# LoRA's transpose behind the output projection, norms 1 and 2 scaled on ScalarE, router logits earlier on VectorE, another form for the row maxima's products

## The chip, the cores and the metric

The kernel runs on one core of a Trainium2 chip. The metric is the device time in microseconds of one execution; lower is better. A core has TensorE (matrix products into PSUM), VectorE, ScalarE and GpSimd (elementwise work; the profile calls them PE, DVE, ACT and POOL), and SyncE (SP), which here issues the DMAs. Each engine runs its own instructions in the order in which they were written, and semaphores tie the engines together.

## The reference

Two layers of cross attention, each followed by a feed-forward part, over x of 8 tiles of 128 tokens by 512. A context of the same size is given. Cut to what matters:

```
x = x + tanh(g0) * xattn_L0(layernorm(x), ctx)     # norm 0; 32 heads, 8 kv heads of 128, rms norm of q and k
x = x + tanh(g1) * lora_ffn(layernorm(x))          # norm 1
x = x + tanh(g2) * xattn_L1(layernorm(x), ctx)     # norm 2; 16 heads, 4 kv heads of 96
x = x + tanh(g3) * swiglu_ffn(layernorm(x))        # norm 3

def lora_ffn(x):                                   # 8 experts of rank 16
    scores = 8 * softmax(x @ Wr.T + br)
    low = einsum('bsd,hrd->bshr', x, A)
    return 2 * einsum('bshr,hor,bsh->bso', low, B, scores)
```

The attention is softmax(q k^T / sqrt(d)) v over 256 keys (128 of the context, 128 of x itself), then the output projection Wo. All is asked for in float32. The kernel keeps the accuracy by splitting each operand into two float16 pieces, high and low, and making three products of them.

## The kernel before

**Tiles and steps.** A group is one kv head pair's share of the weights with NH = 4 query heads; layer 0 has 8 groups and layer 1 has 4, each over the 8 token tiles. That makes N = 96 steps n, 64 of layer 0 (N0) and 32 of layer 1. Each engine has its own function `step(n)`, called in a loop. A pass n works on three steps at once: k, v and q are projected for step T = n + 3; scores, maxima, exponentials and the two pieces of the probabilities are made for S = n + 1; the values product is made for n; the output projection is made for Y = n - 1 (n - 2 in layer 1).

**What runs beside.** `beside(n)` says which tile's norms and LoRA ride along in pass n: norm 1 of tile n - 58, LoRA of tile n - 59, norm 2 of tile n - 60. So LoRA runs in passes 59 to 66, norm 1 in 58 to 65, norm 2 in 60 to 67. Passes 59 and 60 still project for layer 0 (with sums of squares on ScalarE for the rms norms), the ones from 61 on for layer 1.

**A norm.** VectorE takes the statistics (`norm_stats`, L1088 and L1090), GpSimd makes `var_e` and `rstd` (L1473, L1469), VectorE scales `xn` = (x - mean) rstd (`norm_scale`, L1100). For norms 1 and 2 ScalarE copies `xn` into a float16 row tile `n_rows` (`norm_row_hi`, L806), GpSimd puts the rest beside it (`norm_rows`, L1486), and a DMA transposes both into `xT` (`turn_norm`).

**LoRA in a pass.** TensorE projects into bank 2 (`lora_project`, activations and router logits). VectorE makes logits with bias and their maximum (`router_logits`: `lg`, `lmx`), ScalarE the exponential (`router_exp`), VectorE the scaled activations `lora_act` (`lora_scale`, L1235). TensorE transposes them (`lora_turn`, L666), ScalarE and VectorE split the result into `tT_hi` and `tT_lo` (`lora_act_hi`, `lora_low`), TensorE multiplies by B (`lora_project_out`) and VectorE adds to x (`lora_add`, L1246). Bank 2 is the only one for this, so the next pass's `lora_project` waits for `lora_add`.

**Row maxima.** `row_max(n, i)` on VectorE takes the negated maximum over two heads' scores (`mx`, L1180) and multiplies the two columns by a scale into `nb` (L1185 in layer 0, L1189 in layer 1). ScalarE's exponentials (`exps`, L900) use `nb` as bias. VectorE then inverts the sums (`sums_in`, `rs`), and the high and low pieces follow (`probs_high` on ScalarE, `probs_low` on VectorE, `pieces`).

The order of the work is the written order of the calls in each `step(n)`; nothing reorders it.

## Time and profile before

| | us |
|---|---|
| median of 3 runs | 1193.6 |
| lowest, highest | 1191.94, 1197.27 |
| profiled execution, its own time | 1195.74 |
| profiled execution, span | 1193.9 |
| passes before the norms 1 and LoRA come in, one pass of layer 0 | 10.4 |

The page gives for this span: TensorE busy 1133.5 us (95%), VectorE 853.4, ScalarE 825.9, GpSimd 368.6; mean granted TensorE clock 0.986. Busy time alone doesn't say which engine ends a stage, since the engines overlap. What an engine waited for, how long, and what it did in what order tells that; these rows stand further down.

### The profile page before, as it was taken

What the parts mean: (1) busy time and instruction counts of PE and PEld (TensorE: products, weight loads), DVE (VectorE), ACT (ScalarE), POOL (GpSimd) and SP (SyncE); (2) the same over time, 40 slices, a digit from 0 to 9 for tenths busy, and PEclk for the clock granted to TensorE, in tenths of its full rate; (3) what the DMA queues carried; (4) which work ended last, traced back from release to release, by engine and by line L of the source; (5) the groups of instructions that cost most, each with busy time, mean ns of one, the idle gap of its engine ahead of it and who ended that gap; (6) DMA issues with size and microseconds to landing.
All of it is one profiled execution on the core that took longest, in us unless ns stands there. A gap on an engine that the chain in (4) does not pass through costs nothing.

```text
span 1193.9 us, 22716 instructions
## 1 busy us (share of the span) xinstructions
PE 1133.5 (95%) x7184; PEld 712.3 (60%) x7184; DVE 853.4 (71%) x2066; ACT 825.9 (69%) x2695; POOL 368.6 (31%) x668
## 2 busy tenths in 40 slices
PE   6789999999999999999999977899999999799998
PEld 4445666666666666666666544566676766455554
DVE  5578767767777677677676888898887888843434
ACT  5678878888888888878778865577777675522221
POOL 5555333335633333333333543321211121100000
PEclk8899999999999999999999999999999999999999
DMA  6466654464655644555545645568987786200000
GB/s 241 105 141 119 129 137 103 120 137 85 148 123 128 129 101 121 119 109 127 141 95 115 129 96 124 126 136 164 236 182 148 139 159 131 56 1 1 36 1 36
DMA packets 411993, 139.56 MB, mean 117 GB/s; under 512 B 386657, under 2 KB 396641, under 8 KB 411873
## 3 DMA queue, kind: packets, MB, share of 16 engines
q1 hardware_dynamic: 409968, 134.43, 51.1%
q0 software_dynamic: 1904, 3.67, 1.1%
q8 instruction: 58, 0.95, 0.3%
q14 instruction: 63, 0.51, 0.2%
HBM read 39.21 MB, written 2.10 MB: 35 GB/s over the span
## 4 chain that ended last, share of the span: by engine, by line
PE 75%; DVE 9%; SPq 4%; issue 4%; ACT 3%; POOL 3%; DMA 1%; DVEq 0%; POOLq 0%; ACTq 0%
PE bank L517 21%; PE bank L519 21%; PE bank L518 21%; PE bank L718 8%; PE bank L737 4%; SPq L420 1%; DVE mx L1180 1%; DVE stats L1088 1%; ACT probs L900 1%; POOL rstd L1469 1%; DVE pieces L1077 1%; SPq L443 1%; DMA turned<-pieces 1%; SPq L426 1%; SPq L432 1%
## 5 line engine op out<-in xcount | busy, mean ns | idle before, releaser
L806 ACT ACTIVATE pieces<-probs,rs 128x256 f16<-128x256 f32 x384 | 165.3, 524 | 10.6 <-DVE rs L1195 8.4
L1180 DVE TENSOR_REDUCE mx<-bank 128x2 f32<-128x512 f32 x192 | 131.5, 685 | 56.6 <-PE bank L519 56.5
L900 ACT ACTIVATE probs<-bank,nb,rq 128x256 f32<-128x256 f32 x256 | 141.3, 564 | 39.1 <-DVE nb L1185 38.6
L1077 DVE SCALAR_TENSOR_TENSOR pieces<-probs,rs,pieces 128x256 f16<-128x256 f32 x384 | 162.6, 485 | 5.5 <-ACT pieces L806 5.3
L517 PE MATMUL bank<-wo_hi,oT 128*128 128x512 f16 x352 | 135.9, 386 | 6.3 <-DVE oT L1077 4.8
L517 PE MATMUL bank<-wq,xT 128*128 128x512 f16 (+1 forms) x384 | 139.3, 363 | 2.7 <-DVE wq L1077 2.7
L809 ACT ACTIVATE junk<-bank 128x128 bf16<-128x128 f32 x384 | 102.1, 289 | 53.9 <-PE bank L519 53.8
L518 PE MATMUL bank<-wq,xT 128*128 128x512 f16 (+1 forms) x384 | 138.9, 362 | 0.0
L519 PE MATMUL bank<-wq,xT 128*128 128x512 f16 (+1 forms) x384 | 138.7, 361 | 0.0
L519 PE MATMUL bank<-wo_hi,oT 128*128 128x512 f16 x352 | 135.8, 386 | 0.0
L518 PE MATMUL bank<-wo_lo,oT 128*128 128x512 f16 x352 | 135.7, 385 | 0.0
L1077 DVE SCALAR_TENSOR_TENSOR q_rows<-bank,q_rows 128x512 f16<-128x512 f32 (+1 forms) x96 | 61.2, 638 | 79.0 <-ACT junk L809 79.0
L517 PE MATMUL bank<-wkv,xT 128*128 128x256 f16 (+1 forms) x384 | 102.0, 266 | 5.3 <-DVE xT L1074 2.2
L517 PE MATMUL bank<-wkv,cT_hi 128*128 128x256 f16 (+1 forms) x384 | 103.2, 269 | 2.9 <-DVE cT_lo L1077 2.9
L517 PE MATMUL bank<-k_half,q_half 128*128 128x256 f16 (+1 forms) x384 | 105.1, 274 | 0.1
L519 PE MATMUL bank<-k_half,q_half 128*128 128x256 f16 (+1 forms) x384 | 105.2, 274 | 0.0
L518 PE MATMUL bank<-k_half,q_half 128*128 128x256 f16 (+1 forms) x384 | 105.1, 274 | 0.0
L718 PE MATMUL bank<-xT,ff_in 128*128 128x512 f16 x448 | 101.5, 380 | 3.4 <-DVE xT L1074 2.2
L518 PE MATMUL bank<-wkv,cT_hi 128*128 128x256 f16 (+1 forms) x384 | 103.2, 269 | 0.0
L519 PE MATMUL bank<-wkv,cT_lo 128*128 128x256 f16 (+1 forms) x384 | 103.0, 268 | 0.0
L519 PE MATMUL bank<-wkv,xT 128*128 128x256 f16 (+1 forms) x384 | 102.2, 266 | 0.0
L518 PE MATMUL bank<-wkv,xT 128*128 128x256 f16 (+1 forms) x384 | 102.1, 266 | 0.0
(184 smaller groups left out, 2640.7 us busy)
## 6 DMA issues: line engine op xcount, KB each, us to landing
raw_o<-in_wo_a SPq DMA_DIRECT2D x8, 1024.0 KB, 6.1
raw_q<-in_wq_a SPq DMA_DIRECT2D x7, 1024.0 KB, 5.9
raw_kv<-in_wkv_a SPq DMA_DIRECT2D x8, 512.0 KB, 3.9
turned<-pieces SPq DMA_TRANSPOSE x192, 2.8
raw_q<-in_wq_c SPq DMA_DIRECT2D x4, 768.0 KB, 5.1
raw_o<-in_wo_c SPq DMA_DIRECT2D x4, 768.0 KB, 5.1
down_rest<-in_down_t POOLq DMA_DIRECT2D x5, 512.0 KB, 4.2
ff_in<-in_gate_t SPq DMA_DIRECT2D x4, 448.0 KB, 3.9
```

What stands on the lines that cost most here:

```text
L420: sp.dma_start_transpose(turned_in[:, n % 2, i], halves[:, i, :]).then_inc(pturned[i], 16)
L426: sp.dma_start_transpose(q_half[n % 2], q_rows[:, :]).then_inc(qturned, 16)
L517: pe.matmul(out, w[0], m[0], start=start, stop=False)
L518: pe.matmul(out, w[0], m[1], start=False, stop=False)
L519: return pe.matmul(out, w[1], m[0], start=False, stop=stop)
L718: last = pe.matmul(out[:, :], w[:, k, m * P:(m + 1) * P], xT[i][:, k, toks], start=k == 0 and i == 0, stop=k == KC - 1 and i == 1)
L737: last = pe.matmul(bank[t][:, :], hT[n % 2][i][:, t * P:(t + 1) * P], down_w(m), start=m == 0 and i == 0, stop=m == MT - 1 and i == 1)
L806: return act.activation(out, in_, ACT.Copy, scale=scale)
L809: return act.activation(out, in_, ACT.Square, scale=scale, accum_out=total)
L900: act.activation(probs[:, h, :], bank[h // 2][:, (h % 2) * KV:(h % 2 + 1) * KV], ACT.Exp, bias=nb[:, h:h + 1], scale=scale, accum_out=sums ...
L1077: return dve.scalar_tensor_tensor(out, in_, scale, hi, ALU.mult, ALU.subtract)
L1180: dve.tensor_reduce(mx[:, pr], chunks(bank[i][:, :], 2), AX.X, ALU.max, negate=True).then_inc(mx_done, 1)
```

## The change

Four things, all in the calls of the passes and in the helpers they use.

1. TensorE: `lora_turn` stands behind `project(Y)`, no longer ahead of it. ScalarE's `lora_act_hi` and VectorE's `lora_low` move behind the first half of the probabilities' pieces.
2. VectorE: LoRA's logits come before norm 3's scaling (in no pass do both occur), `lora_scale` between the two row maxima and no longer behind both.
3. Norms 1 and 2: VectorE scales them no more. GpSimd makes `shift` = -mean rstd, and ScalarE computes x rstd + shift twice, into `xn` (float32) and into the float16 row tile. Norm 1 stands ahead of norm 2 on GpSimd and in the DMA queue. On ScalarE norm 1's scaling stands right behind `o_hi`, norm 2's behind the router's exponential.
4. `nb` is made with a SCALAR_TENSOR_TENSOR: times 1.0 and times `rq` in layer 0; times `es` plus a tile of zeros in layer 1. This holds for all 192 products.

```diff
@@ TensorE, step
                 if norm3 is not None:
                     norm_turn(3, norm3)
+                if Y is not None:
+                    project(Y)
                 if lora is not None:
                     lora_turn(lora)
-                if Y is not None:
-                    project(Y)
                 values(n)
@@ ScalarE
-            def norm_row_hi(k, t):
-                act.wait_ge(norm[k].xn, t + 1)
+            def norm_scaled(k, t):
+
+                act.wait_ge(norm[k].shift, t + 1)
                 if t >= 1:
+                    act.wait_ge(norm[k].row_lo, t)
                     act.wait_ge(norm[k].moved, 16 * t)
-                copy(rows_slot(k)[:, 0:D], xn[xn_slot(k, t)]).then_inc(norm[k].row_hi, 1)
+                for out, done in ((xn[xn_slot(k, t)], norm[k].xn), (rows_slot(k)[:, 0:D], norm[k].row_hi)):
+                    act.activation(out, xt[:, t, :], ACT.Identity, bias=shift[:, t:t + 1], scale=rstd[:, t:t + 1]
+                                   ).then_inc(done, 1)
@@ ScalarE, step
                     o_hi(n - 1)
+                if norm1 is not None:
+                    norm_scaled(1, norm1)
                 g = kv_squared(n)
...
-                if norm2 is not None:
-                    norm_row_hi(2, norm2)
-                if norm1 is not None:
-                    norm_row_hi(1, norm1)
                 if lora is not None:
                     router_exp(lora)
+                if norm2 is not None:
+                    norm_scaled(2, norm2)
                 if S < N:
                     exps(S, 0)
...
-                if lora is not None:
-                    lora_act_hi(lora)
                 if norm3 is not None:
                     norm_hi(3, norm3)
                 if S < N:
                     probs_high(S, 0)
+                if lora is not None:
+                    lora_act_hi(lora)
+                if S < N:
                     probs_high(S, 1)
@@ VectorE, row_max
-                    dve.tensor_tensor(nb[:, pr], mx[:, pr], rq[:, c:c + 2], ALU.mult).then_inc(nb_done, 1)
+                    dve.scalar_tensor_tensor(nb[:, pr], mx[:, pr], 1.0, rq[:, c:c + 2], ALU.mult, ALU.mult
+                                             ).then_inc(nb_done, 1)
...
-                    dve.tensor_scalar(nb[:, pr], mx[:, pr], es[:, g % 2, s:s + 1], None, ALU.mult).then_inc(nb_done, 1)
+                    dve.scalar_tensor_tensor(nb[:, pr], mx[:, pr], es[:, g % 2, s:s + 1], zeros[:, :], ALU.mult, ALU.add
+                                             ).then_inc(nb_done, 1)
@@ VectorE, step
-                if norm1 is not None:
-                    norm_scale(1, norm1)
-                if norm2 is not None:
-                    norm_scale(2, norm2)
-                if norm3 is not None:
-                    norm_scale(3, norm3)
                 if lora is not None:
                     norms_of_step(n)
                     router_logits(lora)
+                if norm3 is not None:
+                    norm_scale(3, norm3)
                 if S < N:
                     row_max(S, 0)
                 if lora is None:
                     norms_of_step(n)
+                if lora is not None:
+                    lora_scale(lora)
                 if S < N:
                     row_max(S, 1)
-                if lora is not None:
-                    lora_scale(lora)
...
-                if lora is not None:
-                    lora_low(lora)
                 if norm3 is not None:
                     norm_low(3, norm3)
                 if S < N:
                     probs_low(S, 0)
+                if lora is not None:
+                    lora_low(lora)
+                if S < N:
                     probs_low(S, 1)
@@ GpSimd, norm_rstd
                 power(rstd[:, t:t + 1], var_e[:, t:t + 1], half_neg[:, 0:1]).then_inc(norm[k].rstd, 1)
+                if k in (1, 2):
+                    pool.wait_ge(norm[k].rstd, t + 1)
+                    pool.tensor_scalar(shift[:, t:t + 1], moments[:, 2 * t:2 * t + 1], rstd[:, t:t + 1], -1.0,
+                                       ALU.mult, ALU.mult).then_inc(norm[k].shift, 1)
```

Left out are the tiles `shift` and `zeros` with the semaphore `shift`, and the exchange of the calls for norms 1 and 2 on GpSimd and SyncE.

VectorE in pass 61, before, from the end of LoRA's addition in pass 60 on (`x<-bank,tg_lora,x` stands just ahead; `xn` are norms 1 and 2, `mx` and `nb` the row maxima and their products):

```order
L1088 BN_STATS stats<-x 128x6
L1090 BN_AGGR moments<-stats 128x2
L1077 SCALAR_TENSOR_TENSOR oT<-bank,oT 128x512
L1100 TENSOR_SCALAR xn<-x,moments,rstd 128x512 x2
L1114 TENSOR_SCALAR nrm<-bank 128x2
L1223 SCALAR_TENSOR_TENSOR lg<-bank,l_inv,bias_r 128x8
L1226 TENSOR_REDUCE lmx<-lg 128x1
L1180 TENSOR_REDUCE mx<-bank 128x2
L1185 TENSOR_TENSOR nb<-mx,rq 128x2
L1180 TENSOR_REDUCE mx<-bank 128x2
L1185 TENSOR_TENSOR nb<-mx,rq 128x2
L1231 RECIPROCAL lrs<-lsum 128x1
```

and the same place in the changed kernel:

```order
L1084 SCALAR_TENSOR_TENSOR oT<-bank,oT 128x512
L1119 TENSOR_SCALAR nrm<-bank 128x2
L1230 SCALAR_TENSOR_TENSOR lg<-bank,l_inv,bias_r 128x8
L1233 TENSOR_REDUCE lmx<-lg 128x1
L1185 TENSOR_REDUCE mx<-bank 128x2
L1190 SCALAR_TENSOR_TENSOR nb<-mx,rq 128x2
L1238 RECIPROCAL lrs<-lsum 128x1
L1240 TENSOR_SCALAR lg<-lg,lrs 128x8
L1242 TENSOR_TENSOR lora_act<-bank,lg 128x128
L1185 TENSOR_REDUCE mx<-bank 128x2
L1190 SCALAR_TENSOR_TENSOR nb<-mx,rq 128x2
```

The two scalings are gone, the activations' scaling stands one row maximum earlier, and `nb` has the other form.

ScalarE in pass 61, before (`n_rows` are the copies of norms 2 and 1, `probs` the attention's exponentials):

```order
L806 ACTIVATE oT<-bank 128x512
L806 ACTIVATE v_hi<-bank,alpha 128x96 x2
L806 ACTIVATE n_rows_51<-xn 128x512
L806 ACTIVATE n_rows_50<-xn 128x512
L925 ACTIVATE lg,lsum<-lg,lmx 128x8
L900 ACTIVATE probs,sums<-bank,nb,rq 128x256 x4
L806 ACTIVATE q_rows<-bank 128x4x96
L806 ACTIVATE tT_hi<-bank 128x128
L806 ACTIVATE pieces<-probs,rs 128x2x128 x4
```

and in the changed kernel:

```order
L808 ACTIVATE oT<-bank 128x512
L824 ACTIVATE xn<-x,shift,rstd 128x512
L824 ACTIVATE n_rows_50<-x,shift,rstd 128x512
L808 ACTIVATE v_hi<-bank,alpha 128x96 x2
L931 ACTIVATE lg,lsum<-lg,lmx 128x8
L824 ACTIVATE xn<-x,shift,rstd 128x512
L824 ACTIVATE n_rows_51<-x,shift,rstd 128x512
L906 ACTIVATE probs,sums<-bank,nb,rq 128x256 x4
L808 ACTIVATE q_rows<-bank 128x4x96
L808 ACTIVATE pieces<-probs,rs 128x2x128 x2
L808 ACTIVATE tT_hi<-bank 128x128
L808 ACTIVATE pieces<-probs,rs 128x2x128 x2
```

Two copies have become two pairs, norm 1's ahead of `v_hi`, norm 2's between the router's exponential and the attention's; `tT_hi` is now between the halves of the pieces.

## Rows read from the trace of the kernel before

**Rows 1.** Busy time by window, passes before norm 1; columns: us, busy of each engine, clock.

```profile
core 0: us, PE busy (x) PEld busy (x) DVE busy (x) ACT busy (x) POOL busy (x), PEclk, DMA share, GB/s
96.00:656.80 560.80, 559.74 (x3584) 347.98 (x3585) 404.03 (x1013) 463.41 (x1670) 223.36 (x389) 1.00 0.54 120
```

**Rows 2.** The same view, windows from one LoRA addition's end to the next.

```profile
689.24:704.94 15.70, 11.62 (x82) 7.12 (x82) 13.15 (x33) 11.24 (x41) 7.06 (x12) 1.00 0.44 99
704.94:720.33 15.39, 11.95 (x76) 7.06 (x77) 12.51 (x34) 7.21 (x20) 6.00 (x10) 0.89 0.42 95
720.33:734.87 14.54, 11.63 (x93) 7.74 (x91) 12.89 (x33) 10.02 (x28) 4.66 (x8) 1.00 0.56 145
734.87:749.77 14.90, 11.46 (x70) 6.51 (x71) 12.35 (x31) 7.59 (x22) 4.66 (x8) 0.89 0.44 99
749.77:764.75 14.98, 12.55 (x87) 7.83 (x85) 11.91 (x32) 7.17 (x21) 5.67 (x10) 0.89 0.43 98
764.75:777.17 12.42, 9.62 (x86) 7.02 (x84) 10.81 (x30) 8.47 (x24) 4.65 (x8) 1.00 0.66 140
777.17:788.47 11.30, 9.49 (x71) 6.29 (x72) 10.68 (x28) 7.66 (x25) 2.79 (x5) 1.00 0.59 132
```

**Rows 3.** Waits between 678 and 790 us: who for whom, total, times, longest.

```profile
PE bank L666 <- DVE lora_act L1235: 19.1, 7, 3.4
...
DVE xn L1100 <- POOL rstd L1469: 8.2, 7, 1.3
```

**Rows 4.** VectorE's timeline, passes 60 to 61: start, length, instruction, idle before.

```profile
701.43 0.74 DVE L1215 SCALAR_TENSOR_TENSOR x<-bank,ty,x 128x512 f32<-128x512 f32 x1
...
703.54 0.74 DVE L1077 SCALAR_TENSOR_TENSOR wo_lo<-raw_o,s_o,wo_hi 128x512 f16<-128x512 f32 x1
704.20 0.74 DVE L1246 SCALAR_TENSOR_TENSOR x<-bank,tg_lora,x 128x512 f32<-128x512 f32 x1
...
705.71 0.18 DVE L1090 BATCH_NORM_AGGREGATE moments<-stats 128x2 f32<-128x6 f32 x1
705.81 0.66 DVE L1077 SCALAR_TENSOR_TENSOR oT<-bank,oT 128x512 f16<-128x512 f32 x1
707.77 1.00 DVE L1100 TENSOR_SCALAR xn<-x,moments,rstd 128x512 f32<-128x512 f32 x2 [1.30 <-POOL rstd L1469]
...
709.01 0.16 DVE L1226 TENSOR_REDUCE lmx<-lg 128x1 f32<-128x8 f32 x1
...
709.80 0.97 DVE L1185 TENSOR_TENSOR nb<-mx,rq 128x2 f32<-128x2 f32 x1
...
712.26 0.29 DVE L1235 TENSOR_TENSOR lora_act<-bank,lg 128x128 f32<-128x128 f32 x1
...
713.37 0.16 DVE L1193 TENSOR_SCALAR sums_in<-sums 128x4 f32<-128x4 f32 x1
...
714.39 1.67 DVE L1077 SCALAR_TENSOR_TENSOR pieces<-probs,rs,pieces 128x256 f16<-128x256 f32 x4
```

**Rows 5.** ScalarE's timeline, pass 61.

```profile
708.81 1.15 ACT L806 ACTIVATE n_rows<-xn 128x512 f16<-128x512 f32 x2 [4.46 <-DVE xn L1100]
709.87 0.28 ACT L925 ACTIVATE lg<-lg,lmx 128x8 f32<-128x8 f32 x1
...
710.81 0.56 ACT L900 ACTIVATE probs<-bank,nb,rq 128x256 f32<-128x256 f32 x1 [0.57 <-DVE nb L1185]
```

**Rows 6.** GpSimd's timeline, pass 61.

```profile
706.26 0.56 POOL L1469 TENSOR_TENSOR rstd<-var_e,half_neg 128x1 f32<-128x1 f32 x1
...
709.61 2.27 POOL L1486 TENSOR_TENSOR n_rows<-xn,n_rows 128x512 f16<-128x512 f32 x2 [1.87 <-ACT n_rows L806]
```

**Rows 7.** Timelines of VectorE and GpSimd near 69 us, where they overlap.

```profile
68.84 2.65 DVE L1077 SCALAR_TENSOR_TENSOR wo_lo<-raw_o,s_o,wo_hi 128x512 f16<-128x512 f32 x2
...
69.47 1.48 POOL L1486 TENSOR_TENSOR n_rows<-xn,n_rows 128x512 f16<-128x512 f32 x1
```

**Rows 8.** ScalarE's timeline, pass 60.

```profile
690.67 0.62 ACT L806 ACTIVATE v_hi<-bank,alpha 128x128 f16<-128x128 f32 x2
...
695.10 0.56 ACT L900 ACTIVATE probs<-bank,nb,rq 128x256 f32<-128x256 f32 x1 [0.54 <-DVE nb L1185]
```

More of the change, by code:

```diff
@@ L119, in __init__ @@
             self.row_hi = sem("row_hi")
+            self.shift = sem("shift")
             self.row_lo = sem("row_lo")
@@ L206, in build @@
         half_neg = sb("half_neg", NT)
+        zeros = sb("zeros", 2)
         half_pos = sb("half_pos", NT)
@@ L213, in build @@
         stats, moments = sb("stats", NT * 6), sb("moments", NT * 2)
-        var_e, rstd = sb("var_e", NT), sb("rstd", NT)
+        var_e, rstd, shift = sb("var_e", NT), sb("rstd", NT), sb("shift", NT)
         ssq = sb("ssq", C_SUM + len(SETS), BF16)
@@ L451, in step @@
                     turn_norm(0, norm0)
+                if norm1 is not None:
+                    turn_norm(1, norm1)
                 if norm2 is not None:
                     turn_norm(2, norm2)
-                if norm1 is not None:
-                    turn_norm(1, norm1)
                 if T < N:
@@ L946, in step @@
                     o_hi(n - 1)
+                if norm1 is not None:
+                    norm_scaled(1, norm1)
                 g = kv_squared(n)
@@ L1093, in norm_scale @@
                 dve.wait_ge(norm[k].rstd, t + 1)
-                if k in (1, 2) and t >= 1:
-                    dve.wait_ge(norm[k].row_lo, rows_before(k, t))
                 if k in (0, 3) and t >= 2 and turned_by_dma(k, t - 2):
@@ L1272, in step @@
                     context_low(norm0)
-                if norm1 is not None:
-                    norm_scale(1, norm1)
-                if norm2 is not None:
-                    norm_scale(2, norm2)
-                if norm3 is not None:
-                    norm_scale(3, norm3)
                 if lora is not None:
@@ L1612, in step @@
                 next0 = beside(n + 1)[0]
+                if norm1 is not None:
+                    norm_rstd(1, norm1)
                 if norm2 is not None:
                     norm_rstd(2, norm2)
-                if norm1 is not None:
-                    norm_rstd(1, norm1)
                 if norm3 is not None:
@@ L1620, in step @@
                     norm_rows(0, norm0)
+                if norm1 is not None:
+                    norm_rows(1, norm1)
                 if norm2 is not None:
                     norm_rows(2, norm2)
-                if norm1 is not None:
-                    norm_rows(1, norm1)
                 if T < N0:
@@ L1662, in _ @@
             pool.memset(both_half[:, 1:2], 0.5).then_inc(consts, 1)
+            pool.memset(zeros[:, :], 0.0).then_inc(consts, 1)
             pool.memset(kb[:, :], XS * XS * RMS_EPS * L0.hd).then_inc(consts, 1)
@@ L1665, in _ @@
             norm_rstd(0, 1)
-            pool.wait_ge(consts, 8)
+            pool.wait_ge(consts, 9)
             kv_scale(0)
```

## The prediction

> **What bounds the kernel now.** I read the busy time by stage first. Between 96 and 656.8 us TensorE is busy 559.7 of 560.8 us [rows 1]: there the other engines follow, and an edit on them is worth nothing unless it makes TensorE wait. The stretch with LoRA is different. It has eight passes of the step loop, n = 59 to 66. I cut it where LoRA's result has been added (end of the `x<-bank,tg_lora,x` row, L1246), the point that the next pass needs before bank 2 is free. That gives seven lengths, 15.70, 15.39, 14.54, 14.90, 14.98, 12.42 and 11.30 us, together 99.2 [rows 2]. TensorE is busy 78.3 of these, part of that at half clock: the granted clock is 0.89 in three of the seven (2.4 GHz for most of the pass, 1.2 for the rest). So this is the stretch in which 99 us can shrink, and the rest of the kernel offers nothing.
>
> The waits say where it goes [rows 3]: TensorE sat 19.1 us before the transpose of `lora_act` (L666), in seven waits, and VectorE 8.2 us before `xn` for GpSimd's `rstd`. The order on VectorE in pass 61 [rows 4] shows why: after LoRA's addition ends at 704.94 come `oT` (705.81), a wait and the two scalings of norms 1 and 2 (707.77, 1.00 us), the router logits (`lmx` at 709.01), a maximum, the product `nb` (709.80, 0.97 us), and `lora_act` only at 712.26. ScalarE's exponentials of the attention start at 710.81 [rows 5], 5.87 us after the cut. Everything that ends the pass (`pieces`, the output's addition, weights, LoRA's addition) hangs on them and on VectorE's queue.
>
> **The change part by part,** laid out for pass 61 with 704.94 as zero.
>
> (a) VectorE loses the two scalings and the wait ahead of them. After `oT` ends (705.81 + 0.66, so 1.53) the logits and their maximum follow directly. Now they take from the end of `xn` (708.77) to that of `lmx` (709.17), 0.4 us: `lmx` is ready at 1.95. The row maximum needs the first half of the scores. By their shapes at 2.4 GHz LoRA's projection (12 products of 136 columns) takes 0.68 us and half of the scores (6 of 256) 0.64, so they are there by 1.4 to 1.8, in time.
>
> (b) GpSimd: norm 1 goes ahead of norm 2 and each gets one more instruction (`shift`, estimated at 0.3, half of `rstd`'s 0.56). Norm 1's moments are there before the cut. Norm 2's end at 0.95 (705.71 + 0.18 [rows 4]); `rstd` followed by 706.82 [rows 6], so `shift` stands at 2.2. That costs nothing, since ScalarE is busy until then.
>
> (c) ScalarE: the two copies (1.15 us for two, [rows 5]) become two pairs, 2.30. Norm 1's pair runs before `v_hi`, while ScalarE waits anyway. Norm 2's pair stands ahead of the exponentials: router exponential 2.0 to 2.45 (0.28 us and the reading of its sum, [rows 5]), pair 2.45 to 3.6, exponentials from 3.65 instead of 5.87. Identity with two operands per row has no row here; I take the copy's 0.57 each, bounds 0.5 and 0.8 (the second would add 0.5 us a pass).
>
> (d) `nb`. The 0.97 us in [rows 4] is not work: GpSimd's `n_rows` runs from 709.61, 2.27 us for two [rows 6], and `nb` ends with the first. Does the new form escape that? The nearest rows of SCALAR_TENSOR_TENSOR with both inputs in SBUF say no: two `wo_lo` took 2.65 us at 68.84, where one takes 0.74 [rows 4], beside an `n_rows` of 1.48 [rows 7]. So I expect the new form to wait too: the first product ends with norm 1's `n_rows` (GpSimd free for it at 2.2, so near 3.35), hidden behind the scaling pair on ScalarE (3.6). For the 176 products outside the stretch I take 0, since TensorE's own work covers them there [rows 1]; if the cover were gone, each could be longer or shorter by some 0.05. The zeros' memset at the start is behind the load of x: 0.
>
> The trace has the old `nb` held by GpSimd, and held rows of the new form as well. The Trainium skill, "SBUF — State Buffer", section "Who interferes with whom", says that a VectorE instruction with two SBUF inputs contends with a GpSimd instruction that reads SBUF, whatever the opcode; that speaks against this part of the change, and the trace's `wo_lo` agrees. By it the sum stays as it is; were only the old form held, some 3.5 us more would go.
>
> (e) LoRA's scale: now before the second maximum. It needs ScalarE's router exponential (2.45) and VectorE past the first `nb` (3.35); three short instructions, the last of 0.29 [rows 4], estimated at 0.75 together: `lora_act` done at 4.1, the second maximum and `nb` to 5.0, `v_lo` and `kn` to 5.9. The four exponentials end at 3.65 + 4 x 0.56 = 5.9. The two chains meet, neither waits for long.
>
> (f) TensorE: the output projection no longer stands behind the transpose. By the shapes it runs 4.0 to 6.6 at full clock (12 products of 512 columns) and the transpose follows with `lora_act` long there, so that wait goes whole. What is late next: LoRA's last product, now behind `tT_lo`, which has been put behind the first two `pieces`. From `sums_in` to the end of the four `pieces`, `tT_lo` among them, took 713.37 to 716.06, 2.7 us; started at 5.95 and with 0.2 for ScalarE's lead it ends at 8.9, `tT_lo` at 8.05; the product then ends at 8.8 and `v`, `k` of the next pass at 10.8. TensorE then waits about half a us for the addition: VectorE sets the length.
>
> (g) The tail on VectorE, from the y addition to the end of LoRA's: 701.43 to 704.94 is 3.5 us in pass 60, of which `wo_lo` 0.66 (703.54 to the next start) and a `wq` of three quarters of its columns, 0.5, are weights [rows 4]; without them 2.35. So a pass is 8.9 + 2.35 = **11.2 us plus its weights** (o 0.66, q or kv 0.5).
>
> The sum, against the seven lengths [rows 2]:
> - Pass 59 and 60 (layer 0's form, with squares on ScalarE). Here norm 1's pair stands ahead of the squares and `v_hi`. Pass 59 loses up to 1.15, I take 0.6. Pass 60: `v_hi` ended at 691.29; with the pair and the lateness it ends near 693.3, router exponential and norm 2's pair to 694.9, against exponentials that start at 695.10 now [rows 8]. The end of pass 60 comes 0.2 earlier: no more.
> - 61: 11.2 + 0.66 = 11.9, against 15.39: 3.5.
> - 62 (kv, o): 12.35 against 14.54: 2.2.
> - 63 (kv): 11.7 against 14.90: 3.2.
> - 64 (none): 11.2 against 14.98: 3.8.
> - 65 (q, no output's addition and statistics, 1.6; shift late by 0.3): 10.4 against 12.42: 2.0.
> - 66: one `xn` with its wait leaves, exponentials 0.75 earlier, kv projection 0.2 late: 10.75 against 11.30: 0.6.
>
> Together 0.2 + 3.5 + 2.2 + 3.2 + 3.8 + 2.0 + 0.6 = **15.5 us**. The profiled execution took 1195.7 us with a span of 1193.9; the median of the runs is 1193.6, 0.2% less. Taking the gain off the median: **1178 us**. Bounds of the gain: with both products held for a whole `n_rows` each pass (1.1 us, seven passes) and nothing hidden, 8; with the seven passes at VectorE's own work (84.3 busy [rows 2], less 13 scalings of 0.5 and some 6 of held products, 72) 27, which asks that no engine wait for another, so I take 22.
>
> **Rivals.**
> - *The wait only changes its name.* LoRA's last product or its addition becomes what TensorE waits for: `tT_lo` sits later in VectorE's queue than now, and cross-engine hops (0.05 to 0.1 each) that I left out add up to 1 us a pass. Gain 5 to 10, 1186. For it: VectorE is busy 12 to 13 us of every pass even now. Against: 1 us of scaling, 1.3 of waiting and up to 1.1 of held products leave.
> - *The new `nb` is not held.* Then VectorE is ahead of the exponentials and 0.5 us a pass goes, 1174. For it: no row here shows so short an instruction of this form beside `n_rows`. Against: `wo_lo` [rows 7].
> - *Slower: ScalarE's queue.* Norm 2's pair stands ahead of the exponentials and waits for `shift`, thus for GpSimd. If GpSimd comes to norm 2 late (its queue now holds one more instruction per norm ahead) or the pair is dear, all exponentials of the pass wait. The exponentials start at 3.65 by my layout; at 5.87 that gain is gone, and since the rest of pass 61's 3.5 us (1.3, the stall at the transpose and half clock behind it) goes anyway, it turns into a loss from about 7.2. At 8.1, seven passes give +6: 1200. Against: GpSimd is busy only 2.8 to 7.1 us of each pass [rows 2].
> - *It doesn't do what it says:* nothing moves, since the LoRA passes end on something else. Then 1193. Against: 19.1 us of waits on one row.
>
> **Chances.** Forecast (gain 10 to 20) 0.58; wait changes its name 0.18; gain over 20, with the product not held, 0.12; no change 0.07; slower 0.05. The range leaves out the last two and the far ends: 1171 to 1187. A measurement of this kernel tells about 0.5% (6 us) from no change. Faster by more 0.85, within 0.1, slower 0.05.
>
> **What would show it.** Right: the waits before L668's transpose are gone, the clock in the LoRA stretch is 1.00, passes 61 to 64 are 11 to 12.5 us apart and pass 60 is not shorter; `nb` rows beside `n_rows` still reach 0.4 to 1.0 us; steady passes stay at their length. Wrong: TensorE waits 2 us or more a pass for `tT_lo` or for LoRA's addition; exponentials start later than 4.5 us after the cut; or passes before 656 us are longer than before.

## The result, and the profile after the change

| us | before | after |
|---|---|---|
| median of the runs on this chip | 1194.9 (10 runs) | 1188.8 (10 runs) |
| lowest, highest | 1191.94, 1197.27 | 1186.32, 1189.86 |
| profiled execution, its own time | 1195.74 | 1189.01 |
| profiled execution, span | 1193.9 | 1187.2 |

The ratio of after to before is 0.995, with a 95% interval of 0.9939 to 0.9961. The change gains 6 us. The forecast was 15.5, to 1178, with a range of 1171 to 1187: the direction was right, the size wrong by more than half, and the median lies above the range.

The busy time by window, one row for each pass of the LoRA stretch, cut as in [rows 2]. The first window runs from the first row maximum of S = 59 to the end of LoRA's first addition, so it holds most of passes 58 and 59; [rows 2] do not have it. The last row is the stretch of [rows 1].

```profile
core 0: us, PE busy (x) PEld busy (x) DVE busy (x) ACT busy (x) POOL busy (x), PEclk, DMA share, GB/s
667.21:693.22 26.01, 22.09 (x132) 12.57 (x131) 17.32 (x47) 19.82 (x69) 12.19 (x22) 0.93 0.50 114
693.22:708.57 15.35, 12.90 (x96) 8.27 (x94) 11.35 (x31) 12.27 (x41) 8.62 (x16) 1.00 0.40 89
708.57:720.79 12.22, 11.02 (x83) 7.19 (x83) 11.42 (x31) 9.29 (x24) 6.76 (x12) 1.00 0.53 108
720.79:733.82 13.03, 10.94 (x82) 7.11 (x82) 12.22 (x31) 9.79 (x25) 6.02 (x12) 1.00 0.80 184
733.82:747.17 13.35, 10.95 (x82) 7.10 (x82) 11.09 (x29) 10.72 (x28) 5.23 (x10) 1.00 0.45 102
747.17:759.00 11.83, 11.03 (x84) 7.33 (x84) 11.04 (x29) 8.68 (x23) 5.87 (x13) 1.00 0.50 112
759.00:770.37 11.37, 8.03 (x53) 5.10 (x54) 10.41 (x26) 10.34 (x27) 4.75 (x9) 0.90 0.96 181
770.37:782.95 12.58, 12.05 (x99) 8.83 (x96) 10.23 (x27) 8.40 (x24) 3.06 (x6) 0.96 0.50 111
...
96.00:656.80 560.80, 559.73 (x3584) 347.95 (x3585) 404.05 (x1012) 462.84 (x1670) 222.69 (x389) 1.00 0.53 120
```

The same view of the kernel before, first window alone:

```profile
667.35:689.25 21.90, 21.70 (x143) 13.06 (x140) 18.69 (x49) 16.14 (x60) 10.92 (x18) 1.00 0.62 136
```

The passes of layer 0 are what they were. Passes 61 to 65 are shorter, as forecast, though less so. But passes 58 and 59 together are 4.1 us longer (26.01 against 21.90), and pass 66 is 12.58 us where it was 11.30. Half clock has become rarer and has moved: TensorE has it for 3.4 us each from 689.5 and 768.0 us (the second lies across two windows), where the kernel before has it three times, in the three windows of [rows 2] with 0.89.

The waits between 678 and 790 us, the stretch of [rows 3] (who waits for whom, total, times, longest):

```profile
POOL var_e L1477 <- DVE moments L1097: 37.4, 15, 5.1
ACT xn L824 <- POOL shift L1483: 21.6, 8, 3.1
...
POOL n_rows L1494 <- ACT n_rows L824: 15.0, 10, 3.2
PE bank L519 <- DVE tT_lo L1081: 11.7, 8, 3.7
...
PE bank L668 <- DVE lora_act L1242: 0.2, 1, 0.2
```

The first row is nothing new: before the change `var_e` waited 44.3 us. TensorE's 19.1 us before the transpose have become 0.2. In their place stand 11.7 us before LoRA's last product, which needs `tT_lo`, and 21.6 us in which ScalarE stands before `xn` for GpSimd's `shift`. Before, `tT_lo` held TensorE for 0.2 us in all, and `shift` did not exist.

ScalarE's timeline of passes 58 and 59 after the change (start, length, instruction, idle before):

```profile
667.26 0.81 ACT L824 ACTIVATE xn<-x,shift,rstd 128x512 f32<-128x512 f32 x1 [2.73 <-POOL shift L1483]
...
671.33 0.56 ACT L906 ACTIVATE probs<-bank,nb,rq 128x256 f32<-128x256 f32 x1
...
680.71 0.81 ACT L824 ACTIVATE xn<-x,shift,rstd 128x512 f32<-128x512 f32 x1 [3.00 <-POOL shift L1483]
681.43 0.80 ACT L824 ACTIVATE n_rows<-x,shift,rstd 128x512 f16<-128x512 f32 x1
...
682.63 0.61 ACT L808 ACTIVATE v_hi<-bank,alpha 128x128 f16<-128x128 f32 x2
...
683.42 0.57 ACT L906 ACTIVATE probs<-bank,nb,rq 128x256 f32<-128x256 f32 x1
```

and of the kernel before:

```profile
668.27 0.56 ACT L900 ACTIVATE probs<-bank,nb,rq 128x256 f32<-128x256 f32 x1
...
680.08 0.56 ACT L900 ACTIVATE probs<-bank,nb,rq 128x256 f32<-128x256 f32 x1 [1.09 <-DVE nb L1185]
```

VectorE's first row maximum of S = 60, which opens pass 59, after the change and before it:

```profile
680.55 0.68 DVE L1185 TENSOR_REDUCE mx<-bank 128x2 f32<-128x512 f32 x1
```

```profile
678.37 0.69 DVE L1180 TENSOR_REDUCE mx<-bank 128x2 f32<-128x512 f32 x1
```

The scaling of norm 1 waits 2.73 us in pass 58 and 3.00 us in pass 59. Behind it, in ScalarE's own queue, stand `v_hi` and the exponentials. Counted from the start of the window (667.21 after, 667.35 before), the exponentials of pass 58 start at 4.12 us, against 0.92 before, the first maximum of S = 60 at 13.34, against 11.02, and the exponentials of pass 59 at 16.21, against 12.73. So 2.3 us of the delay arise in pass 58 and 1.2 more in pass 59.

### The profile page after: what moved, and what is told of

It is laid out like the page before. It is cut to its first block, busy times and chain, and to the rows that moved or that the text cites. A ratio compares the mean times of both kernels' runs of the same rounds, so it can differ in the third digit from the quotient of the medians.

```text
span 1187.2 us, 22719 instructions
## 1 busy us (share of the span) xinstructions
PE 1129.7 (95%) x7184; PEld 712.0 (60%) x7184; DVE 844.7 (71%) x2050; ACT 836.9 (70%) x2711; POOL 374.2 (32%) x685
## 4 chain that ended last, share of the span: by engine, by line
PE 79%; DVE 9%; ACT 5%; issue 3%; POOL 2%; DMA 1%; DVEq 0%; POOLq 0%; ACTq 0%
PE bank L519 22%; PE bank L520 22%; PE bank L521 22%; PE bank L720 8%; PE bank L739 4%; ACT probs L906 2%; DVE pieces L1084 2%; DVE stats L1095 1%; DVE mx L1185 1%; DVE x L1222 1%; ACT junk L811 1%; POOL rstd L1473 1%; DVE q_rows L1084 0%; DVE nb L1195 0%; DVE nb L1190 0%
## 5 line engine op out<-in xcount | busy, mean ns | idle before, releaser
L519 PE MATMUL bank<-wo_hi,oT 128*128 128x512 f16 x352 | 133.4, 379 | 6.0 <-DVE oT L1084 4.6
L521 PE MATMUL bank<-wo_hi,oT 128*128 128x512 f16 x352 | 133.4, 379 | 0.0
L520 PE MATMUL bank<-wo_lo,oT 128*128 128x512 f16 x352 | 133.4, 379 | 0.0
## 6 DMA issues: line engine op xcount, KB each, us to landing
raw_q<-in_wq_c SPq DMA_DIRECT2D x4, 768.0 KB, 5.0
raw_o<-in_wo_c SPq DMA_DIRECT2D x4, 768.0 KB, 5.1
```

Source lines behind the costliest of these rows:

```text
L519: pe.matmul(out, w[0], m[0], start=start, stop=False)
L520: pe.matmul(out, w[0], m[1], start=False, stop=False)
L521: return pe.matmul(out, w[1], m[0], start=False, stop=stop)
```

## The experiments

Lengths in us of each pass, cut as above, then the sum from the first row maximum of S = 59 to that of S = 70 (with the stretch behind pass 66 in it), each from one profiled execution. The first column of lengths holds passes 58 and 59.

| kernel | 58, 59 | 60 | 61 | 62 | 63 | 64 | 65 | 66 | sum |
|---|---|---|---|---|---|---|---|---|---|
| before | 21.9 | 15.7 | 15.3 | 14.6 | 15.0 | 15.0 | 12.3 | 11.4 | 139.9 |
| after | 26.0 | 15.4 | 12.2 | 13.0 | 13.4 | 11.8 | 11.4 | 12.6 | 134.9 |
| a1_pair_behind_v | 23.3 | 15.3 | 12.2 | 12.7 | 12.0 | 11.5 | 10.9 | 12.4 | 129.6 |
| a2_old_product | 26.0 | 15.4 | 12.2 | 13.0 | 13.3 | 11.8 | 11.4 | 12.4 | 134.8 |
| a3_low_ahead | 26.0 | 15.4 | 14.1 | 12.8 | 13.8 | 11.7 | 10.9 | 11.0 | 134.8 |
| b1_turn_alone | 21.9 | 15.7 | 14.2 | 14.7 | 14.1 | 13.5 | 12.8 | 11.6 | 137.3 |
| c1_both_pairs_late | 23.3 | 17.9 | 14.5 | 14.1 | 13.5 | 12.7 | 12.1 | 12.5 | 143.6 |
| c2_norms_alone | 25.4 | 15.4 | 12.2 | 12.7 | 13.2 | 11.5 | 10.8 | 10.6 | 131.2 |
| c3_vector_order | 22.6 | 15.3 | 13.5 | 14.0 | 13.4 | 12.9 | 11.8 | 11.5 | 133.8 |
| c4_all_but_norms | 22.6 | 15.3 | 13.7 | 14.2 | 13.6 | 13.1 | 12.0 | 13.4 | 136.7 |
| d2_all_but_turn | 26.0 | 15.4 | 12.0 | 12.8 | 13.2 | 11.7 | 10.9 | 11.9 | 133.4 |
| d3_pair_and_turn | 23.3 | 14.6 | 12.0 | 13.0 | 12.0 | 11.7 | 10.5 | 11.0 | 127.2 |
| d4_low_ahead_in_65 | 23.3 | 15.4 | 12.2 | 12.7 | 12.1 | 11.5 | 10.5 | 11.1 | 127.9 |
| d5_k_norm_ahead | 23.3 | 15.0 | 12.0 | 13.0 | 11.9 | 11.3 | 10.5 | 11.0 | 127.1 |

**a1_pair_behind_v**: the changed kernel with norm 1's pair moved down ScalarE's queue.

```diff
                     o_hi(n - 1)
-                if norm1 is not None:
-                    norm_scaled(1, norm1)
...
                     v_hi(T)
+                if norm1 is not None:
+                    norm_scaled(1, norm1)
```

> The changed kernel, but norm 1's scaling on ScalarE stands behind v_hi (ahead of the router's exponential) and no longer right behind o_hi. Theory Q (ScalarE's queue): in passes 58 to 60 the pair that waits for shift holds up the squares and v_hi and so the attention's exponentials, 1.7 us in pass 58 and 3.3 us in pass 59; most of that comes back, 3 to 5 us, ratio to the kernel before 0.991 to 0.992. Theory L (the late low piece): what is lost is TensorE's wait for tT_lo, so this moves nothing, 0.995. Theory P (the pair's own length, 1.5 us instead of the 1.15 that was forecast): nothing moves, 0.995, since both pairs stay ahead of the exponentials.

Measured: 1183.8 us, ratio 0.9909 (0.9886 to 0.9931). ScalarE at the place shown above:

```profile
679.17 0.81 ACT L824 ACTIVATE xn<-x,shift,rstd 128x512 f32<-128x512 f32 x1 [0.27 <-POOL shift L1483]
...
680.88 0.54 ACT L906 ACTIVATE probs<-bank,nb,rq 128x256 f32<-128x256 f32 x1
```

The wait is 0.27 instead of 3.00, because what stood behind the pair now runs in that time; over the stretch ScalarE waits 4.5 us for `shift`, where it waited 21.6. The exponentials of pass 59 start 12.87 us into the window (680.88, window from 668.01) instead of 16.21. The stretch is 5.3 us shorter than in after; passes 58 and 59 give 2.75 of that and pass 63 gives 1.3. The first maximum of S = 60 starts 11.16 us into the window (13.34 after, 11.02 before), so pass 58 has nearly its whole loss back. The place of norm 1's pair is a cause of the miss, and the largest one found. In pass 63 two `wq` of 0.83 us each (ScalarE's sums of squares of the weights) stood behind the waiting pair as well.

**a2_old_product**: the changed kernel with `nb` in its two old forms.

```diff
-                    dve.scalar_tensor_tensor(nb[:, pr], mx[:, pr], 1.0, rq[:, c:c + 2], ALU.mult, ALU.mult
+                    dve.tensor_tensor(nb[:, pr], mx[:, pr], rq[:, c:c + 2], ALU.mult).then_inc(nb_done, 1)
```

> The changed kernel with the row maxima's products in the old form (TENSOR_TENSOR in layer 0, TENSOR_SCALAR in layer 1). If the new form is held by GpSimd as the old one is, the ratio stays at 0.995 within 0.001, and the product's rows beside n_rows are still 0.4 to 1.1 us. If the new form gave something, the time rises by 1 to 3 us.

Measured: 1189.5 us, ratio 0.9956 (0.9939 to 0.9973), the same as after. In pass 63 both forms are held by GpSimd. VectorE's and GpSimd's timelines of the changed kernel:

```profile
736.29 0.87 DVE L1195 SCALAR_TENSOR_TENSOR nb<-mx,es,zeros 128x2 f32<-128x2 f32 x1
735.99 1.16 POOL L1494 TENSOR_TENSOR n_rows<-xn,n_rows 128x512 f16<-128x512 f32 x1
```

VectorE's timeline in a2:

```profile
735.58 0.88 DVE L1194 TENSOR_SCALAR nb<-mx,es 128x2 f32<-128x2 f32 x1
```

In the stretch the form is worth nothing (134.8 and 134.9 us). Outside it no difference stands clear of the noise.

**b1_turn_alone**: before, with only the transpose and the split of its result moved, as the change does.

```diff
-                if lora is not None:
-                    lora_turn(lora)
                 if Y is not None:
                     project(Y)
+                if lora is not None:
+                    lora_turn(lora)
```

> The kernel before with one part of the change alone: the transpose of lora_act behind the output projection, and the high and low pieces of it behind the first half of the probabilities' pieces. Theory: the wait of TensorE at the transpose (19.1 us) goes, the clock stays at 1.00, but the exponentials start where they did, so the passes are set by VectorE's queue: passes 61 to 64 become 13.5 to 14 us instead of 14.5 to 15.4, 5 to 8 us in all, ratio 0.994 to 0.996. Rival: the wait only changes to tT_lo, 0.998 to 1.0.

Measured: 1192.2 us, ratio 0.9987 (0.9977 to 0.9997). Its waits:

```profile
PE bank L517 <- DVE tT_lo L1075: 7.6, 6, 2.3
PE bank L666 <- DVE lora_act L1236: 6.9, 6, 3.4
```

Of the 19.1 us on `lora_act` [rows 3] 12.2 are gone, and 7.6 on `tT_lo` have come. Alone, the move gains about 2 us, and the ratio lies in the rival's range: the wait in the main changes its place.

**a3_low_ahead**: the changed kernel with `lora_act_hi` and `lora_low` back ahead of the pieces on ScalarE and VectorE, the transpose still behind the projection.

```diff
+                if lora is not None:
+                    lora_low(lora)
                 if norm3 is not None:
                     norm_low(3, norm3)
                 if S < N:
                     probs_low(S, 0)
-                if lora is not None:
-                    lora_low(lora)
```

> The changed kernel with the high and low pieces of the transposed activations back ahead of the probabilities' pieces (the transpose itself stays behind the output projection). Theory L: TensorE's wait for tT_lo (11.7 us in eight waits) shrinks by about 0.8 us in each, 2 to 4 us of the time, 0.992 to 0.993. Theory Q and P: VectorE sets the passes anyway and TensorE's wait moves to LoRA's addition, within 1 us, 0.995.

Measured: 1187.6 us, ratio 0.995 (0.9932 to 0.9968), no difference from after. The wait moves to ScalarE, here in pass 61, where `tT_hi` waits for the late transpose with the pieces behind it:

```profile
715.06 0.28 ACT L808 ACTIVATE tT_hi<-bank 128x128 f16<-128x128 f32 x1 [1.92 <-PE bank L668]
715.23 1.69 ACT L808 ACTIVATE pieces<-probs,rs 128x256 f16<-128x256 f32 x4
```

So `tT_lo` isn't late through its place alone; with a late transpose neither place is free. The equal time hides two changes, by the table: passes 61 and 63 are 1.8 and 0.5 us longer than in the changed kernel, passes 65 and 66 are 0.5 and 1.6 shorter.

**c1_both_pairs_late**: a1, and norm 2's pair moved behind the exponentials too.

```diff
-                if norm2 is not None:
-                    norm_scaled(2, norm2)
                 if S < N:
...
                     exps(S, 1)
+                if norm2 is not None:
+                    norm_scaled(2, norm2)
```

> The changed kernel with norm 1's pair behind v_hi (as in a1) and norm 2's pair behind the attention's exponentials. Theory P (the pair of 1.5 us in front of the exponentials is on the path): the exponentials of passes 60 to 67 start 1 to 1.5 us earlier, 4 to 8 us less than a1, ratio to the kernel before 0.984 to 0.988. Rival: VectorE's own queue sets the passes, then within 2 us of a1, 0.989 to 0.991.

Measured: 1197.7 us, ratio 1.0039 (1.002 to 1.0058): slower than before, and 14 us slower than a1. GpSimd's timeline in pass 60:

```profile
699.02 1.15 POOL L1494 TENSOR_TENSOR n_rows<-xn,n_rows 128x512 f16<-128x512 f32 x1 [3.93 <-ACT n_rows L824]
700.40 0.71 POOL L1473 TENSOR_TENSOR kr<-kvar,half_neg 128x2 f32<-128x2 f32 x1
```

VectorE's timeline there:

```profile
701.15 0.61 DVE L1169 SCALAR_TENSOR_TENSOR kn<-bank,kr,k_weight 128x128 f32<-128x128 f32 x2 [4.40 <-POOL kr L1473]
```

GpSimd waits 3.93 us for the late pair, its `kr` stands behind that, and VectorE waits 4.40 for `kr` with the pieces behind it: pass 60 takes 17.9 us. Behind the exponentials is a worse place for norm 2's pair than ahead of them. The passes behind 60 are longer than in a1 as well, and those I didn't follow one by one; between 688 and 800 us GpSimd waits 37.6 us for the late row tiles, where in a1 it waits 9.8, and TensorE 3.8 us for the transposed rows `xT`, where in a1 it waits 0.8.

**c2_norms_alone**: before, with only the norms changed: `shift` on GpSimd, both pairs on ScalarE where the change puts them, norm 1 first. Old order on VectorE, old `nb`, transpose ahead of the projection.

```diff
                     o_hi(n - 1)
+                if norm1 is not None:
+                    norm_scaled(1, norm1)
...
-                if norm2 is not None:
-                    norm_row_hi(2, norm2)
-                if norm1 is not None:
-                    norm_row_hi(1, norm1)
                 if lora is not None:
                     router_exp(lora)
+                if norm2 is not None:
+                    norm_scaled(2, norm2)
```

> The kernel before with one part of the change alone: shift on GpSimd, norms 1 and 2 scaled on ScalarE in the places of the change, norm 1 first. Transpose, LoRA's order on VectorE and the products are as before. Theory Q: passes 58 to 60 lose the 4 us that they lose in the whole change, passes 61 to 65 win about 2 us each because VectorE has no scalings, in all 0.995 to 0.999. Rival (the norms on ScalarE bring nothing at all): 1.002 or more.

Measured: 1184.2 us, ratio 0.992 (0.9903 to 0.9937): one part of the change gains more than the whole of it, and the intervals don't meet. That is better than either of the two ranges that I had written down. Waits of TensorE:

```profile
PE bank L668 <- DVE lora_act L1239: 9.2, 7, 2.8
...
PE bank L519 <- DVE tT_lo L1080: 1.3, 2, 1.1
```

By the table passes 60 to 64 are as long as in the whole change, within 0.4 us; passes 65 and 66 are 2.6 us shorter.

**c3_vector_order** and **c4_all_but_norms**: before, with the order of VectorE alone (logits ahead of the scalings, LoRA's scale between the maxima, norm 1 first, the router's exponential ahead of the copies); and the same with the transpose behind the projection as in b1.

```diff
                     context_low(norm0)
+                if lora is not None:
+                    norms_of_step(n)
+                    router_logits(lora)
                 if norm1 is not None:
...
-                if S < N:
-                    row_max(S, 1)
                 if lora is not None:
                     lora_scale(lora)
+                if S < N:
+                    row_max(S, 1)
```

> The kernel before with VectorE's order alone: router logits ahead of the scalings of norms 1 and 2, LoRA's scaling between the two row maxima, the router's exponential ahead of ScalarE's copies, norm 1 ahead of norm 2 everywhere. Theory: lora_act comes 1.5 to 2 us earlier, TensorE's wait at the transpose falls from 19.1 us by about 10, but the attention's exponentials start as late as before, so the time falls less, 0.995 to 0.998. Rival (the transpose's wait was the path): 10 us, 0.992.

> c3 with the transpose behind the output projection too: everything of the change but the norms on ScalarE (and the products' form). Theory Q: nothing is lost in passes 58 to 60; passes 61 to 66 keep the scalings on VectorE, 13.5 us each; 0.993 to 0.996, so the norm part of the change as it was made is worth about nothing. Rival: the norms on ScalarE carry the gain, then this stays at 0.998 or more.

Measured: c3 1189.3 us, 0.9958 (0.9943 to 0.9973); c4 1191.4, 0.9974 (0.9961 to 0.9987). The order on VectorE alone gives as much as the whole change. With the transpose behind the projection the time isn't shorter but rather 2 us longer, 2.8 in the traces' sums (133.84 and 136.66), and c4 falls between its theory's range and its rival's. TensorE's waits for `lora_act` fall from 8.1 to 1.6 us, those for `tT_lo` rise from 2.0 to 14.1.

**d2_all_but_turn** and **d3_pair_and_turn**: the changed kernel, and a1, with the transpose and its split in the places of before (the edit of b1 the other way round).

> The changed kernel with the transpose (and the high and low pieces behind it) back in its old place ahead of the output projection; norms, LoRA's order on VectorE and the products' form as changed. Theory T: once lora_act comes early, the transpose behind the output projection and the low piece behind the probabilities' pieces only make TensorE wait in its last LoRA product (11.7 us, half clock at 689 and 768 us); taken back, pass 66 falls from 12.6 to about 10.6 us and the total by 3 to 5 us, 0.991 to 0.992. Rival: the norms alone (0.992) were ahead of the whole change by chance and LoRA's order on VectorE costs it, then this stays at 0.995.

> d2 and a1 together: transpose in its old place, norm 1's pair behind v_hi. If the two losses (ScalarE's queue in passes 58 and 59, the late transpose in 65 and 66) are separate, they add: 0.986 to 0.988, and this beats both kernels. If they are the same wait seen twice, it stays with a1 at 0.991.

Measured: d2 1186.9 us, 0.9932 (0.9917 to 0.9947), against after's 0.995; d3 1181.1, 0.9882 (0.9865 to 0.9898), against a1's 0.9909. Each interval touches its partner's, but all three pairs (c3 with c4, d2 with after, d3 with a1) point the same way, by 2 to 3 us, and the traces' sums by 1.4 to 2.8; 1.1 to 2.1 of that lie in passes 65 and 66. d3 is at the edge of the range that was forecast for separate losses, d2 gains less than its theory said. d2 is also c2 with LoRA's order on VectorE and the new `nb` on top: it is no faster than c2 (0.9932 and 0.992, intervals that overlap). With the scalings gone from VectorE, LoRA's order there shows no gain of its own.

**d4_low_ahead_in_65**: a1, and in pass 65 alone, which has no output projection (Y is None), `tT_hi` and `tT_lo` ahead of the pieces.

```diff
+                if lora is not None and Y is None:
+                    lora_low(lora)
                 if S < N:
                     probs_low(S, 0)
-                if lora is not None:
+                if lora is not None and Y is not None:
                     lora_low(lora)
```

> a1 with one difference: in pass 65 alone, which has no output projection, the high and low pieces of the transposed activations stand ahead of the probabilities' pieces. In a1 TensorE waits for tT_lo there, the clock falls to 0.5 at 763.3 us and pass 66 takes 12.4 us. If that wait is the cause, pass 66 falls to 10.6 to 11.2 and the total by 1 to 2 us, 0.989 to 0.990; if pass 66 is set by something else, nothing moves.

Measured: 1181.7 us, 0.9888 (0.9873 to 0.9902). TensorE's timeline at LoRA's last product in pass 65, and the busy time of the window behind it, first of the changed kernel:

```profile
768.12 0.61 PE L519 MATMUL bank<-lb_hi,tT_hi 128*128 128x512 f16 x1 [3.23 <-DVE tT_lo L1081]
768.00:771.40 3.40, 3.28 (x16) 2.30 (x17) 3.11 (x8) 2.87 (x7) 0.00 (x0) 0.50 1.01 74
```

the same of a1:

```profile
763.76 0.61 PE L519 MATMUL bank<-lb_hi,tT_hi 128*128 128x512 f16 x1 [2.77 <-DVE tT_lo L1081]
763.30:766.70 3.40, 2.94 (x14) 2.02 (x15) 3.14 (x7) 3.22 (x8) 0.00 (x0) 0.50 1.16 82
```

and of d4:

```profile
762.13 0.39 PE L519 MATMUL bank<-lb_hi,tT_hi 128*128 128x512 f16 x1 [1.80 <-DVE tT_lo L1083]
...
763.30:766.70 3.40, 3.39 (x42) 3.06 (x41) 3.30 (x9) 2.86 (x8) 0.69 (x2) 1.00 0.75 114
```

After waits of 3.23 and 2.77 us the granted clock is 0.50 (1.2 GHz) and a product of 512 columns takes 0.61 us; after 1.80 it stays 1.00 (2.4 GHz) and the product takes 0.39. Passes 65 and 66 together go from 23.3 us in a1 to 21.6. By the times alone a1 and d4 can't be told apart.

The length of the wait doesn't decide alone. Here are TensorE's transpose in pass 60 of the kernel before, and LoRA's last product of pass 65 in d2:

```profile
696.90 0.33 PE L666 MATMUL bank<-ident,lora_act 128*128 128x128 f32 x1 [2.81 <-DVE lora_act L1235]
```

```profile
766.02 0.39 PE L519 MATMUL bank<-lb_hi,tT_hi 128*128 128x512 f16 x1 [2.26 <-DVE tT_lo L1080]
```

The first was followed by full clock (the window of pass 60 has 1.00 in [rows 2]), the second by half clock from 767.1 us on, 1 us after the wait. In a3 that product waits 2.26 us too, and the clock stays full. The clock also differs between executions of one kernel: a1's four had mean clocks of 0.988, 0.994, 0.993 and 0.988 at 1185.0, 1181.0, 1182.5 and 1185.0 us, and the first of them is the profiled one. So how much of the 1.7 us is the edit's and how much that execution's is not shown.

**d5_k_norm_ahead**: d3 with GpSimd's `k_norm` ahead of norm 2's `n_rows`.

```diff
-                if norm2 is not None:
-                    norm_rows(2, norm2)
                 if T < N0:
                     k_norm(T)
+                if norm2 is not None:
+                    norm_rows(2, norm2)
```

> d3 with one exchange on GpSimd: the k norm (kvar, kr) of layer 0 ahead of norm 2's n_rows. It touches pass 60 alone, where VectorE waits about 1.6 us for kr behind n_rows, which waits for ScalarE's pair. If that wait is on the path, pass 60 falls from 15.4 to 14 us and the total by 1 us; otherwise it is equal to d3 within the measurement.

Measured: 1181.5 us, 0.9885 (0.987 to 0.99), no difference from d3, and pass 60 is 15.0 us, in d3 14.6. The 1.6 us that I expected to remove are the changed kernel's; in d3 VectorE waits 0.4 us for `kr`, so there was hardly anything to win. The chain through `kr` that c1 showed is short when the pairs come early.

The fastest versions are d3, d4 and d5, 1.1 to 1.2% below before and more than twice the change's gain.

## Why the prediction was wrong, step by step

From the first maximum of S = 59 to that of S = 70 the traces differ by 5.0 us, where 15.5 were forecast. The forecast length less the measured one, per pass: passes 58 and 59 -3.5; 60 -0.5; 61 -0.3; 62 -0.7; 63 -1.65; 64 -0.6; 65 -1.0; 66 -1.8; together -10; 0.3 more lie behind pass 66. Another 1.5 us of the span's gain lies behind S = 70, where of the change only the new `nb` runs. That part is 385.0 to 386.3 us long in the eight kernels with the new `nb` and 385.8 to 387.0 in the six with the old one; alone, an `nb` of layer 1 takes 0.22 us in the new form and 0.23 in the old. Scatter and a small effect of the form can't be told apart here.

- **(c), the step that failed: "Norm 1's pair runs before `v_hi`, while ScalarE waits anyway."** I placed the pair in ScalarE's idle time and didn't ask when its own input arrives. `shift` is made by GpSimd behind VectorE's moments. ScalarE's queue is in order, so squares, `v_hi`, `wq` and exponentials stood behind a wait of up to 3.1 us, 21.6 in all between 678 and 790 us. The sum gave pass 59 a loss of 0.6, at most 1.15, and had no term for pass 58, which carries norm 1 too. Passes 58 and 59 together lost 4.1: the exponentials of pass 59 came 3.5 us late, 2.3 of it through pass 58 and 1.2 through pass 59 itself, so for pass 59 alone the bound was about right, and most of the loss was in the pass left out. The idle time of [rows 5] (4.46 us) was itself a wait for the norms; moving the work to another engine doesn't make its input earlier. a1 shows it: 2.75 us come back in passes 58 and 59, 1.3 in 63.
- **(c), the price of a pair.** I took 1.15 us, from the copies' row, and it is 1.52: 0.81 and 0.80, with 0.72 from start to start. The upper bound I had named, 0.8 each, was the true one. In pass 61 it didn't delay the exponentials, since norm 2's pair started 2.30 us after the cut, where 2.45 was forecast; what it delays is norm 2's `n_rows` on GpSimd (see (e), the second product). The Trainium skill, "ScalarE: Activation LUTs", section "What ACT_TABLE_LOAD costs", gives for an ACTIVATE 186 ns + 0.833 ns per column and about 93 ns more for each operand of [128,1]: 0.80 us for 512 columns with two of them. The trace agrees, with 0.80 and 0.81 us.
- **(f), the wait that took the other's place.** That the transpose's wait "goes whole" was right (0.2 us left). But I took "about half a us" for what TensorE then waits. It waited 11.7 us in eight passes for `tT_lo`, 1.5 a pass, at worst 3.7. With two of these waits, 3.71 us in pass 59 and 3.23 in pass 65, came half clock. Behind the second, pass 66 took 12.58 instead of 10.75, and VectorE stood 1.44 us for LoRA's logits there. For pass 65 I counted only what the missing output step saves on VectorE. The output projection is also work that could have covered the wait for `tT_lo` (argued, not run). What is shown is that with the split ahead of the pieces in pass 65 the wait shrinks to 1.80 us in d4 and 2.26 in a3, the clock stays full, and pass 66 takes 11.1 and 11.0 us. This is the rival "the wait only changes its name", which had 0.18, with a gain of 5 to 10; the measured 6 is in it. Its mechanism was one part of the truth, ScalarE's queue the other, so that the number fits it is in part luck.
- **The gain that I gave to the turn.** Once `lora_act` is early, the transpose hardly waits in its old place: 3.7 us in d2, and in d3 it is not among the waits of TensorE. Then its move has nothing left to gain, and puts a short chain (transpose, `tT_hi`, `tT_lo`, last product) at the end of the pass. The parts don't add: alone against before the move gains 2 us, on top of the rest it costs 2 to 3. In (f) I took the wait as gone and gave no price to that chain.
- **(a), (b) and the first half of (e)** held in substance in pass 61: `lora_act` ends 4.0 us after the cut, where 4.1 was forecast. Its exponentials start at 712.28, 3.71 us after the cut, where 3.65 was forecast, and the pass is 12.22 against 11.9. But in passes 60, 63 and 66 they start 5.55, 5.36 and 5.12 us after the cut, later than the 4.5 that I had named as a sign of being wrong. `shift` took 0.26 for 0.3. What missed in (b) is the end of `rstd`, not of `shift`, in passes where VectorE's weights run beside it (last section).
- **(d)** held for the first product: the new form is held as the old one is (0.81 us in pass 61, 0.87 in pass 63), and a2 shows no worth in it. "The new `nb` is not held" is refuted. The Trainium skill's rule on two SBUF inputs in "SBUF — State Buffer", "Who interferes with whom", agrees for the new form and for the old one of layer 0. The old one of layer 1 has one such input and a scalar, so that rule doesn't speak of it; in a2 it took 0.88 us beside `n_rows`.
- **(e), the second product.** I had it unheld, with the four exponentials back to back. In pass 61 it takes 0.49 us beside norm 2's `n_rows`, and the third exponential waits for it. VectorE, GpSimd and ScalarE:

```profile
713.23 0.49 DVE L1190 SCALAR_TENSOR_TENSOR nb<-mx,rq 128x2 f32<-128x2 f32 x1
```

```profile
712.55 1.15 POOL L1494 TENSOR_TENSOR n_rows<-xn,n_rows 128x512 f16<-128x512 f32 x1 [0.64 <-ACT n_rows L824]
```

```profile
713.75 0.56 ACT L906 ACTIVATE probs<-bank,nb,rq 128x256 f32<-128x256 f32 x1 [0.28 <-DVE nb L1190]
```

The last exponential ends 6.3 us after the cut instead of 5.9, the `pieces` 9.3 instead of 8.9. Had the pair taken 1.15 us, this `n_rows` would end some 0.37 earlier and hold the product for less time (an estimate from these rows, not run).
- **The slower rival** named the right engine and the wrong norm. Its mechanism, exponentials behind a pair that waits for `shift`, is what norm 1's pair did, for 3.5 us by pass 59. That its chain can end on the slower side is what c1 shows, though by an opposite move.
- **The steady passes** stayed at 559.73 busy of 560.80, as forecast.

a1's edit and d4's together bring the stretch from 134.9 to 127.9 us, 7.0 of the 10 that were missed. Of the other 3, 0.8 lie in passes 58 and 59 and the rest in all the others but 65, 0.3 to 0.5 us each. It isn't a later start of the exponentials: in d4 they start 3.68 to 3.81 us after the cut in each of the passes 61 to 66, and the `pieces` end at 9.2 to 9.3 where 8.9 was forecast. Read from the traces, in these passes it is the second product and, behind it, the pair's price; no run takes either away. Open is why the clock falls where it does between kernels that are nearly alike: d2 has it at 685.2, 709.1 and 767.1 us, c2 at no place in the stretch.

## What to carry to other kernels

An idle engine is a place for work only if the work's inputs are there when the idle time begins: before moving an instruction up an in-order queue, find out who releases it and list what stands behind it. Of two cures for one wait (earlier data, later consumer), price the second again with the first in place, since the later consumer then only lengthens the end of the chain. And a pass that lacks a step is not only shorter: look for the wait that this step used to cover.

## What the runs showed of the hardware

Being held goes both ways, and very small instructions are held too. GpSimd's `var_e` and `rstd` of one column took 0.46 and 0.94 us beside VectorE's `wq` and `wo_lo`, where 0.19 and 0.56 are usual. GpSimd's timeline after the change:

```profile
706.84 0.46 POOL L1477 TENSOR_SCALAR var_e<-moments 128x1 f32<-128x1 f32 x1 [2.21 <-DVE moments L1097]
707.38 0.94 POOL L1473 TENSOR_TENSOR rstd<-var_e,half_neg 128x1 f32<-128x1 f32 x1
708.42 0.26 POOL L1483 TENSOR_SCALAR shift<-moments,rstd 128x1 f32<-128x1 f32 x1
709.60 0.19 POOL L1477 TENSOR_SCALAR var_e<-moments 128x1 f32<-128x1 f32 x1 [0.92 <-DVE moments L1097]
709.88 0.56 POOL L1473 TENSOR_TENSOR rstd<-var_e,half_neg 128x1 f32<-128x1 f32 x1
```

VectorE's at the same time:

```profile
706.66 0.58 DVE L1084 SCALAR_TENSOR_TENSOR wq<-raw_q,s_q,wq 128x384 f16<-128x384 f32 x1
707.16 0.74 DVE L1084 SCALAR_TENSOR_TENSOR wo_lo<-raw_o,s_o,wo_hi 128x512 f16<-128x512 f32 x1
```

`var_e` began inside `wq` and ended 0.06 us behind it; `rstd` began inside `wo_lo` and ended 0.42 behind. Norm 2's, the last two rows, ran at their usual pace. That one held the other is read from the overlap; no experiment here took the overlap away. But the trace has both cases many times. Between 30 and 805 us after the change, `var_e` takes 0.46 us six times and 0.59 once, each time beside a VectorE weight instruction with both tensors in SBUF (`wq`, `wkv` or `wo_lo`), and `rstd` 0.94 and 0.95 beside `wo_lo`. Beside instructions of the same form whose one input is in PSUM (`oT<-bank,oT` and `x<-bank,tg_lora,x`), and with nothing beside them, `var_e` takes 0.19 and `rstd` 0.55 to 0.56 every time. So in these rows not every SCALAR_TENSOR_TENSOR holds GpSimd, only those with both tensors in SBUF.
